# Half-precision parts of each head side by side, and expert tiles moved next to the dense experts

## The reference: what is computed

```python
x = x + ln(attn0(ln(x)))   # causal attention, 16 heads of 8, relative-key bias
x = x + ln(ffn0(ln(x)))    # silu(gate) * up, 384 hidden, weights from int32
x = x + ln(attn1(ln(x)))   # quaternion projections, q and k normed, 16 heads of 8, no mask:
                           #   softmax(q k^T * scale + const) v
x = x + ln(moe(ln(x)))     # 8 experts, the 2 best per token:
                           #   probs = softmax(x gate^T); sum_k p_k (gelu(x w1_e + b1_e) w2_e + b2_e)
```

## Time and profile before

| | |
|---|---|
| median of 3 runs | 1028.57 us |
| profiled execution | 1028.42 us |
| its span, first to last instruction | 1026.6 us |
| granted TensorE clock, mean | 0.914 |
| PE, DVE, ACT, POOL busy | 788.0, 558.1, 486.0, 288.4 us |
| chain that ended last, by engine | PE 49%, DVE 26%, issue 9%, ACT 8%, POOL 3% |

### The profile page before, as it was taken

How to read it: one execution, slowest core, us unless ns; L and a number is a source line. 1 busy time by engine, 2 the same in 40 slices (tenths; PEclk the granted TensorE clock), 3 DMA queues, 4 the chain that set the end, 5 groups by cost and what they waited for, 6 DMA issues and landing times.

```text
span 1026.6 us, 21722 instructions
## 1 busy us (share of the span) xinstructions
PE 788.0 (77%) x8393; PEld 567.9 (55%) x8393; DVE 558.1 (54%) x1728; ACT 486.0 (47%) x1035; POOL 288.4 (28%) x366
## 2 busy tenths in 40 slices
PE   1688886778887889888989786976667576765896
PEld 0577765656665566665566552754426453365575
DVE  3255566466655374545374724776645366298145
ACT  1234352325544547754557525778343365434332
POOL 3200101000333020233020234553273675046400
PEclk9989999799998999997999988999876788889899
DMA  4400200001100001000001011010110110101100
GB/s 122 135 2 2 117 2 3 1 1 28 38 2 11 2 12 42 2 23 12 9 5 32 12 40 44 27 34 12 49 52 23 47 47 8 34 28 36 40 11 21
DMA packets 32530, 29.89 MB, mean 29 GB/s; under 512 B 9230, under 2 KB 26404, under 8 KB 32300
## 3 DMA queue, kind: packets, MB, share of 16 engines
q1 hardware_dynamic: 30636, 25.23, 8.6%
q0 software_dynamic: 1536, 3.15, 1.1%
q10 hardware_dynamic: 256, 0.13, 0.0%
HBM read 11.44 MB, written 8.52 MB: 19 GB/s over the span
## 4 chain that ended last, share of the span: by engine, by line
PE 49%; DVE 26%; issue 9%; ACT 8%; POOL 3%; ACTq 1%; another core or an unknown queue 1%; POOLq 0%; SPq 0%; DMA 0%; DVEq 0%
PE ps L1522 5%; PE ps L1667 5%; PE ps L1537 4%; PE ps L1682 4%; PE ps L1525 4%; PE ps L1450 3%; PE ps L1550 3%; PE ps L1767 3%; PE ps L1758 3%; DVE probsT L973 3%; PE ps L1617 2%; PE ps L1519 2%; ACT late L901 2%; DVE neg_max L1160 2%; DVE stats L1006 2%
## 5 line engine op out<-in xcount | busy, mean ns | idle before, releaser
L901 ACT ACTIVATE late<-ps,j_bias 128x512 f32<-128x512 f32 x256 | 173.6, 693 | 193.6 <-PE ps L1667 170.7
L1160 DVE TENSOR_REDUCE neg_max<-ps 128x2 f32<-128x32 f32 (+31 forms) x128 | 90.4, 706 | 148.2 <-PE ps L1528 144.1
L611 POOL TENSOR_SCALAR q_heads<-q_heads,head_mask 128x512 fp32r<-128x512 f32 x64 | 100.6, 1588 | 206.0 <-DMA q_heads<-q_half 205.9
L1667 PE MATMUL ps<-q_heads,k_parts 128*128 128x512 f32 x256 | 138.7, 558 | 17.1 <-ACT late L901 14.1
L828 ACT ACTIVATE probs<-ps,neg_max 128x16 f32<-128x16 f32 (+31 forms) x256 | 108.9, 483 | 26.5 <-DVE neg_max L1160 26.2
L752 ACT ACTIVATE probsT<-ps 128x128 f32<-128x128 f32 (+3 forms) x128 | 55.8, 436 | 127.3 <-PE ps L1537 113.7
L1522 PE MATMUL ps<-kT_two,q_wide 64*64 64x262 f32 (+16 forms) x1024 | 74.2, 354 | 36.3 <-DVE probsT L973 24.7
L973 DVE COPY probsT<-ps 128x128 f32<-128x128 f32 (+3 forms) x173 | 74.8, 432 | 48.2 <-PE ps L1537 24.8
L1537 PE MATMUL ps<-ident,probs 128*128 128x128 f32 x640 | 97.5, 284 | 1.0 <-ACT probs L828 1.0
L635 POOL TENSOR_TENSOR q_wide<-qT,eighth_mask 128x1024 f32<-128x1024 f32 x16 | 31.2, 1948 | 228.8 <-PE ps L1528 167.6
L1667 PEld LDWEIGHTS ps<-q_heads,k_parts 128*128 128x128 f32 x256 | 50.8, 206 | 66.6 <-ACT late L901 45.2
(11 more groups left out here) (259 smaller groups left out, 1424.4 us busy)
## 6 DMA issues: line engine op xcount, KB each, us to landing
k_parts<-k_half SPq DMA_DIRECT2D x64, 64.0 KB, 2.0
q_heads<-q_half SPq DMA_DIRECT2D x64, 64.0 KB, 2.0
x_by_expert<-q_heads SPq DMA_DIRECT2D x3, 960.0 KB, 7.6
probsT<-x_by_expert SPq DMA_DIRECT2D x45, 64.0 KB, 1.8
y_by_expert<-probsT SPq DMA_DIRECT2D x45, 64.0 KB
late<-in_L_ffn_w_dram SPq DMA_DIRECT2D x1, 2048.0 KB
w_in<-in_L_ffn_w_dram SPq DMA_DIRECT2D x1, 2048.0 KB
x_all<-in_L_attn_x_dram SPq DMA_DIRECT2D x4, 256.0 KB, 5.3
```

The costliest lines, as they stand in the source:

```text
L611: last = pool.tensor_scalar(q_heads[:, hg % 2, g, :], together.bitcast(f32), head_mask[:, g:g + 1], None, ALU.mult)
L901: nc.scalar.activation(head_probs[:, i % SLOTS, :], ps[:, banks[i % len(banks)], :], ACT.Exp, bias=j_bias[:]).then_inc(e2_ready.sem, 1)
L1160: nc.vector.tensor_reduce(neg_max[:, n % 4, :], ps[:, k:k + OCT, 0:QS * (n + 1)], axis=AXX, op=ALU.max, negate=True).then_inc(max_ready.se ...
L1667: mm(ps[:, banks[i % R], :], k_parts[:, hg, kc * P:(kc + 1) * P], q_heads[:, hg % 2, g, :], start=True, stop=True).then_inc(s2_ready.sem, 1)
```

## The change

1. **Spreading.** The four copies of a group are laid on neighbouring partitions (`parts[c:P:4]`): row i of the group lies on partitions 4i to 4i+3. A head's 8 rows with their four products are then 32 partitions in a row, and one matmul over these 32 partitions gives the same sum. `q_parts` has room for all four groups. POOL's masks, `head_mask`, the stage Q on SP and POOL and the signal `heads_apart` go. SP waits for both q_half and k_half before the first group, then issues 8 transfers a group; S has two pieces in place of four.
2. **The plan.** In round 4, N of batch 1 stands at slot 8 in place of 45, F of batch 3 at 23 in place of 8, its S at 61 and 63; X of batch 1 begins at slot 54 of round 4 in place of slot 12 of round 5, and ends at slot 26 of round 5. C of batches 0 and 1 lies in round 5. In the tail only the first two pieces of X of batch 2 stand beside N; the others stand beside D, three behind each of D's pieces, and C of batch 2 beside D's last three.
3. **Gelu.** For batch 2 (`BY_GELU`) ACT takes the gelu straight from the up product; DVE's and ACT's operations for the tanh form go.
4. **Banks of D.** Up products use banks 0 and 5 (two, not three), down products 6 and 7.

```diff
-    NUP = 3
+    UP_BANKS, DOWN_BANKS = (0, 5), (6, 7)
+    NUP = len(UP_BANKS)
+    BY_GELU = LAST - 1
@@ plan
-                put(r, 6 + late, "F", f, 37)
+                put(r, 23, "F", f, 37)
-                put(r, 45, "N", 1, 15)
+                put(r, 8, "N", 1, 15)
                 put(r, 16, "X", 0, NX, 2)
+                put(r, 54, "X", 1, NX, 2)
             if q - 1 == 2:
                 put(r, 8, "N", 2, 15)
-                put(r, 12, "X", 1, NX, 2)
-                put(r, 24, "C", 0, 1)
-                put(r, 44, "C", 0, 2)
+                put(r, 2, "C", 0, 1)
+                put(r, 26, "C", 0, 2)
+                put(r, 38, "C", 1, 1)
+                put(r, 58, "C", 1, 2)
@@ tail
-        for k in range(max(NX, RANKED)):
-            if k < RANKED:
-                yield ("N", LAST)
-            if k < NX:
+        for k in range(RANKED):
+            yield ("N", LAST)
+            if k >= RANKED - 2:
                 yield ("X", LAST - 1)
         for k in range(NE):
             yield ("D", LAST)
-            if k in (0, 2, 3):
-                yield ("C", LAST - 2)
-            if k in (1, 4, 5):
+            yield from [("X", LAST - 1)] * 3
+            if k in (5, 6, 7):
                 yield ("C", LAST - 1)
@@ sync
+            def spread_group(b, hg):
                 if b:
                     sp.wait_ge(s2_ready.sem, s2_ready.at(b - 1, (hg + 1) * GH * KC))
                 for c in range(4):
+                    for half, parts, which, done in ((k_half, k_parts, c // 2, k_spread), (q_half, q_parts, c % 2, q_spread)):
+                        sp.dma_start(parts[c:P:4, hg, :].bitcast(f32),
+                                     half[hg * GR:(hg + 1) * GR, which, :].bitcast(f32)).then_inc(done[hg].sem, 16)
@@ scalar, by_expert
-                                                        ps[:, 1 + (b * NT + n) % 2, m * P:(m + 1) * P], ACT.Identity,
+                                                        ps[:, 1 + (b * NT + n) % 2, m * P:(m + 1) * P],
+                                                        ACT.Gelu_apprx_tanh if b == BY_GELU else ACT.Identity,
@@ tensor, quat
-                        mm(ps[:, banks[i % R], :], k_parts[:, hg, kc * P:(kc + 1) * P], q_heads[:, hg % 2, g, :],
+                        rows = slice(g * GR, (g + 1) * GR)
+                        mm(ps[:, banks[i % R], :], k_parts[rows, hg, kc * P:(kc + 1) * P], q_parts[rows, hg, :],
                            start=True, stop=True).then_inc(s2_ready.sem, 1)
```

More of the change, by code:

```diff
@@ L185, in build_sandwich @@
         signs = sb("signs", [P, 4])
-        head_mask = sb("head_mask", [P, GH])
         eps_col = sb("eps_col", [P, 1])
@@ L495, in spread @@
                 sp.wait_ge(k_half_ready.sem, k_half_ready.at(b, 1))
+                sp.wait_ge(q_half_ready.sem, q_half_ready.at(b, 1))
                 for hg in range(HG - 1):
[L497 to L499 removed]
+                    spread_group(b, hg)
                 yield
[L501 to L511 removed]
+                spread_group(b, HG - 1)
                 yield
@@ L553, in all_experts @@
                 yield
-            take({"S": spread, "Q": quat, "X": by_expert, "C": sums, "D": all_experts})
+            take({"S": spread, "X": by_expert, "C": sums, "D": all_experts})
             sp.wait_ge(x_stored.sem, x_stored.at(B, 0))
@@ L601, in _ @@
                                allow_small_or_imprecise_dtypes=True))
-            step(pool.tensor_tensor(out=head_mask[:], in0=eighth_mask[:, 0:GH], in1=eighth_mask[:, GH:QB],
-                                    op=ALU.add))
-            step(pool.tensor_scalar(head_mask[:], head_mask[:], 0.0, None, ALU.is_gt))
             pool.memset(signs[0:1, 0:1], 1.0).then_inc(consts_ready, 1)
-            def heads(b, hg):
-                pool.wait_ge(q_spread[hg].sem, q_spread[hg].at(b + 1, 0))
-                together = q_heads[:, hg % 2, 0, :]
-                for g in (1, 2, 3, 0):
-                    last = pool.tensor_scalar(q_heads[:, hg % 2, g, :], together.bitcast(f32),
-                                              head_mask[:, g:g + 1], None, ALU.mult)
-                last.then_inc(heads_apart.sem, 1)
-            def spread(b):
-                yield
-                heads(b, 0)
-                yield
-                yield
-                heads(b, 1)
-                yield
-            def quat(b):
-                for hg in range(2, HG):
-                    for _ in range(22 if hg == 2 else GH * KC):
-                        yield
-                    heads(b, hg)
-                yield
             def relative(b):
@@ L717, in sums @@
                 yield
-            take({"R": relative, "A": attention, "W": weights, "S": spread, "Q": quat, "N": norm, "X": by_expert,
-                  "C": sums})
+            take({"R": relative, "A": attention, "W": weights, "N": norm, "X": by_expert, "C": sums})
         def copy_pT(eng, copy, o, done, b, n):
@@ L922, in by_expert @@
                     n = j - 2
-                    if 0 <= n < NT:
+                    if 0 <= n < NT and b != BY_GELU:
                         act.wait_ge(hv_ready.sem, hv_ready.at(b, n + 1))
@@ L1742, in by_expert @@
                     if 0 <= n < NT:
-                        pe.wait_ge(hx_ready.sem, hx_ready.at(b, n + 1))
+                        if b == BY_GELU:
+                            pe.wait_ge(hb_ready.sem, hb_ready.at(b, n + 1))
+                        else:
+                            pe.wait_ge(hx_ready.sem, hx_ready.at(b, n + 1))
                         if b * NT + n:
@@ L1780, in all_experts @@
                 for t in range(T):
-                    last = mm(ps[:, 3, t * P:(t + 1) * P], gates_T[:, t, :], b2_sb[:], start=True, stop=True)
+                    last = mm(ps[:, DOWN_BANKS[1], t * P:(t + 1) * P], gates_T[:, t, :], b2_sb[:], start=True, stop=True)
                 last.then_inc(accb_ps.sem, 1)
                 for e in range(NE):
+                    yield
                     if e + 1 < NE:
```

75 lines of the change are left out of this document (27 added, 48 removed).

## The result

The changed kernel takes 1076.49 us (median of 4 runs, 1069.1 to 1080.39), the kernel before 1030.05 in the same comparison: a ratio of 1.045 (1.038 to 1.051). It is slower by 46 us, where the prediction had it 12 faster. The profiled execution took 1069.1 us, its span is 1067.2, the mean clock 0.872.

What follows compares the result with a forecast made beforehand. It took the first attention to rule four rounds, stalls behind busy POOL to hold PE in round 5, and PE to bound D. Round 5 -26.5, round 4 +14.5, spreading +2, scores +5, tail -7: -12, 1016 us (1000 to 1032).

Steps and rivals of the forecast that it cites:

- The score matmul: 32-row score blocks: one more shape change at 0.09 us for each of 128 blocks, half on the path; +5 us.
- Rival 4: Row tiles drain the array at both sides of each of 256 blocks: 46 us in place of 5, 1057 us; chance 0.08.
- Masks: POOL's 64 masks go; only one stall from them, 7.3 us in round 5, was on the path.
- Spreading ... hidden ... +2 (0 to 6): SP's 24 transfers at slot 61 take 15 us, first group hidden, later row loads a little late; +2 us.
- Slots 27 to 63: Round 5: 37 slots at 0.85 us plus batch 1's sum, no tile behind its gather; 36 us.
- The scatter in round 4: Round 4: batch 1's scatter on POOL, between tiles 2 and 3 of batch 0, makes a new wait of 10 us.
- F ... now 18 lie beside it: +3.5: Round 4: F ran beside 15 tiles' pieces in 87.2 us; with 18 it takes 3.5 us more.
- What was to be gained in round 5: Round 5 between first and last exponential: 111 us against 137.4, a gain of 26.5 us.
- The tail: From N of batch 3 to the end: -12 us, with 5 given back by C of batch 2; -7 us.
- rival 2: Tail: tiles beside the experts keep their ring, 3.29 us each in place of 2.3; 15 us more, 1031 us; chance 0.1.
- Rival 1: POOL waits hide better: round 4's scatter (-10) and C of batch 2 (-5); 1001 us; chance 0.2.
- Rival 3: Round 5's saving fails: masks not on the path, N with eight tiles takes 5 us more; 1026 us; chance 0.12.

Runs made afterwards that it cites:

- e1: The changed kernel with each score product of the second attention contracting over all 128 rows again; 1034.97 us, ratio 1.006 to the kernel before.
- e9: e4 without POOL's 64 masks; 1013.93 us, ratio 0.986 to the kernel before.
- e4: The kernel before with the new tail alone; 1024.05 us, ratio 0.994 to the kernel before.
- e3: The changed kernel with the order of rounds 4 and 5 as before, 32-row scores and new tail kept; 1054.98 us, ratio 1.023.
- e12: e1 with the spreading of batch 3 issued one group at a time, 8 transfers each, in place of 24 and 8; 1026.11 us, ratio 0.995.
- f1: The kernel of e5 run once more, unchanged; 995.89 us, ratio 0.970 to the kernel before.
- e11: e1 with F, N and spreading of round 4 back in their old slots and batch 1's tiles begun at slot 60; 1016.42 us, ratio 0.989.
- e10: e5 with a 32-row, 32-column product put ahead of each full score product, which overwrites it; 1075.98 us, ratio 1.044 to the kernel before.
- e8: The changed kernel with a 128-row, 256-column product added ahead of each 32-row score product in rounds 4 and 5; 1080.08 us, ratio 1.056.
- e7: The changed kernel with each score product over 64 rows; 1036.13 us, ratio 1.009 to the kernel before.
- e5: e3 with scores contracted over all 128 rows (old order, new tail, no masks); 996.55 us, ratio 0.971 to the kernel before.
- f3: Old order, new tail, no masks, zero-padded heads over full rows, the second half of q's transfers spread four at a time; 996.88 us, ratio 0.971.

## Why the prediction was wrong

It forecast -12 and +46 came: 58 us off. Two terms hold 57 of them.

**The score matmul: +5 forecast, 40 measured** (the ratios of after and e1; the profiled executions, of which after's is its fastest, lie 33 apart). The step that failed is "about one change more for each of 128 blocks, half of them on the path ... and almost nothing later, where PE waits anyway", in its count and in half of its price. The price of leaving was read rightly, 0.09 from the earlier trace rows against 0.08 here; that of entering, 0.17 behind a product on the full array, was not looked at, though the rows of the kernel before show the 0.04 that it would be held against. In rounds 2 and 3 the changed kernel is 17.6 us longer than e1, 0.14 a slot: PE is busy 292.8 us in place of 265.9, and only 9.3 of these 26.9 us are hidden in its waits. And "almost nothing later" was wrong: rounds 4 and 5 gave 16.7 us more (PE is busy 29 us longer, 12.4 of them hidden) while their time at the lower clock rose from 116 to 173 us, which no term had. How the 16.7 divide between the changes of tile and the clock is not shown. Rival 4 was the nearest, with 1057 us. Its mechanism, paid on both sides of each block, is the one that the starts show, and its 2 x 0.09 is near the measured 0.2, though it took both sides as alike. (The prediction points to it as the second-last rival; it is the last.) Its chance of 0.08 rested on PE's waiting in rounds 4 and 5, which covers less than half. The Trainium skill, "TensorEngine Tiling (Array Packing)", Key Properties, names the drain; the runs agree, and they put 0.08 to 0.2 us on it.

**Rounds 4 and 5: -10 forecast, masks and spreading among it.** Measured: the masks -9 (e9 against e4), the order +21 (e1 at 1.006 against e9 at 0.986; after against e3, which differ by the order alone, give 22), together +12. With the row tiles' 40 and the tail's -6 that is the +46. By its steps:

- Masks, 7.3: right.
- "Spreading ... hidden ... +2 (0 to 6)": 10.6 (e12 against e1). This step failed: the sum looked at the group that PE needs, and not at the row loads queued behind. The first 8 slots of round 5 took 31.6 us in place of 19.4. The busy time of ACT's L853 in the stretches of round 5, which answer to the earlier trace rows:

```profile
799.00:830.60 31.60, 5.49 (x8) 0.73 0.29 78
830.60:883.70 53.10, 12.71 (x19) 0.78 0.08 23
883.70:932.40 48.70, 22.81 (x38) 0.59 0.10 29
```

- Slots 8 to 26, forecast 45 + 10.5: 53.1, right. Slots 27 to 63, forecast 36: 48.7 here, at a clock of 0.59, and 42.2 in e1. The step "the gather of batch 1 has no tile behind it" failed: no tile waits for it, but ACT stands while POOL issues it (884.9 to 894.7), and PE behind ACT. Who waited for whom from 884 to 899:

```profile
ACT late L853 <- remote: 11.5, 1, 11.5
PE ps L1624 <- ACT late L853: 11.0, 1, 11.0
```

  In e1 PE's wait at this place is 10.6, in e12 11.0; f1, e9 and the kernel before have no such wait of ACT's in round 5 (the last section says what is known of such waits).
- The scatter in round 4, forecast 10: right in size, 7.3 here and 10.6 in e1. POOL's scatter stands ahead of the tile's weights, and PE waits (rows of who waited for whom, rounds 4 and 5; the first row is the wait just named and smaller ones, the third stands beside the gather of batch 0, the last one is a late row load):

```profile
PE ps L1624 <- ACT late L853: 15.8, 7, 11.0
PE ps L1695 <- issue: 7.3, 1, 7.3
PE ps L1513 <- issue: 5.1, 1, 5.1
...
PE ps L1687 <- DMA probsT<-x_by_expert: 3.2, 1, 3.2
```

- "F ... now 18 lie beside it: +3.5": e11, which puts F and N back, is 1.7% or 17 us under e1, and 29.6 in slots 0 to 59. Slots 4 to 59 of round 4 hold all of F, N of batch 1 and the tiles of batch 0 in both kernels; e1 has the first three pieces of batch 1's tiles in them besides. First e1, then e11 (busy times, then who waited for whom, of the same slots):

```profile
617.40:768.40 151.00, 102.39 (x585) 68.16 (x585) 86.51 (x281) 77.51 (x162) 43.82 (x84) 0.84 0.07 20
```

```profile
612.70:734.70 122.00, 92.39 (x558) 60.09 (x557) 79.81 (x270) 77.64 (x156) 29.30 (x60) 0.91 0.11 29
```

```profile
PE ps L1359 <- DVE xn L991: 19.2, 3, 8.5
PE ps L1695 <- POOL probsT L654: 10.6, 1, 10.6
```

```profile
PE ps L1359 <- DVE xn L991: 12.6, 3, 5.7
PE ps L1687 <- DVE probsT L927: 6.7, 5, 2.1
```

  Of the 29 us between them the scatter is 10.6, and 18 stay where 3.5 were forecast (about 4 of them, at the prediction's 1.3 a tile, for the three pieces). F's head, whose norms are a serial chain on DVE, ran before the first tile and now runs among tiles (PE's waits for it, 12.6 and 19.2 us); and PE takes 10.0 us more for 585 products in place of 558, at a clock of 0.84 in place of 0.91. How the rest divides between these two is not shown.
- What was to be gained in round 5, 26.5, came as 9.1 in e1 and 17.5 in e12. The 17.4 that e1 lacks are SP's queue (8.4, the way from e1 to e12) and ACT's wait beside the gather (10.6), which together are a little more than it.

**The tail: -7 forecast, -6.8 in the traces, -6 by e4.** Its parts held but for N alone, 24.1 us (935.0 to D's first product) where 19.5 and a tile's first products were forecast. PE from one expert to the next, with three tiles between, which answers to the earlier trace rows:

```profile
972.66 3.79 PE L1718 MATMUL ps<-xnT,w1T 128*128 128x512 f32 x8
976.28 3.73 PE L1729 MATMUL ps<-w2T,late 128*128 128x128 f32 x32
979.85 0.27 PE L1687 MATMUL ps<-ident,probsT 128*128 128x128 f32 x1
...
986.80 3.79 PE L1718 MATMUL ps<-xnT,w1T 128*128 128x512 f32 x8
```

14.1 us, forecast 14; rival 2, the tiles keeping their ring, is out. DVE did wait for C of batch 2 before the last two sums:

```profile
1050.08 0.88 DVE L1313 TENSOR_SCALAR q_rel<-q_wide,top_p 128x128 f32<-128x128 f32 x4 [6.52 <-DMA q_wide<-y_by_expert,row_no]
```

Rival 1 is out: of the two waits, the scatter was not hidden and C of batch 2 not either. Rival 3 (what is saved in round 5 isn't saved) had the right direction for the wrong reason: the masks were on the path, and it was SP and the wait beside the gather, and in the changed kernel the clock as well, that took the gain.

## What to carry to other kernels

Price a smaller contraction by its entries and exits, each time that its neighbours on TensorE have another tile shape, and read both from the starts, before and behind the block (here 0.2 to 0.25 us a block, of which leaving is less than half); where zeros can be laid down once, padding to full rows keeps the shape, at the price of more and smaller transfers that have to be spread out (here 16 a group). When work is moved out of a round with slack into one beside a serial chain, the engines that run their lists in order (DVE here, and SP's queue) carry the new delays, so look at what is queued behind each moved piece, and what must come before it (e11's first tile and its scatter), and not only at whether the piece itself is in time. And idle time of TensorE is weak cover: of the 29 us that PE was busy longer in rounds 4 and 5, where it had waited 95 us in e1, 12.4 were hidden.

## What the runs showed of the hardware

- The lower clock can last while PE is busy: 57.8 of 60 us in e10, 90 of 105 in e8, 45 of 50 in the changed kernel. All of these have 32-row tiles among products on full rows; in the kernels with full score products and nothing added no such stretch exceeds 23.9 us. That 32-row products bring it about is shown by the pairs that differ in them (low time 214 against 136, 228 against 123, 200 against 119) and that short ones suffice by e10; what in them does (the drains, the share of cells at work, or in e10 the added product as such) isn't.
- 32-row tiles cost 4% of this kernel. 64-row tiles have the same prices of entering and leaving in e7's trace; what they cost in all is not shown, since e7 (1.009) and e1 (1.006) ran with different waits of the kind below, and e7's eleven executions spread from 1032 to 1058 us.
- Leaving a 32-row tile costs 0.08 us, entering one behind a product on the full array 0.17; behind a group of products on 64x64 tiles entering costs nothing more (a block starts 0.14 us after the last of them in either kernel). A 32-row product of 32 columns delays a full one by 0.21 us, where a small full-array product takes 0.11.
- ACT and DVE can stand while POOL's indirect transfers are issued, for up to 19 us, with a releaser that the profile can't name:

```profile
ACT late L853 <- remote: 29.4, 2, 17.9
DVE outT L927 <- remote: 11.9, 1, 11.9
```

These rows are the changed kernel's (17.9 at the start of round 4 beside the scatter of batch 0, 11.5 in round 5 beside the gather of batch 1); before has such waits too (19.5 and 12.0 us), as have e1 to e4 and e9 to e12. e5 to e8 and f1 to f3 have none, and their first four exponentials of round 4 take 12 to 17 us in place of 21 to 25. e5's kernel lacked them both times, but so did others run beside it, and the kernel before was 3 to 5 us faster there (1026 in place of 1029 to 1031 us). By f1's expectation its outcome (no such wait, 0.970) would make them the kernel's own; but e10, which is e5's kernel with one product more, has the wait, and e7 and e8, which have the changed kernel's order, lack it. So they seem to belong to the execution, and up to 1% of the distance between e9 and f1, which differ by the layout of the spreading, may be theirs. That is why the order's cost was taken against e9. Part of that cost, the 10.6 us beside the gather of batch 1, is such a wait. Their cause is open.
